# A fused AdaLN block with a mixture of experts: low parts of the bias rows on VectorE, and new hand-written orders at both ends

## The reference

```
mod = silu(c) @ wmod                      # per batch: sa, ca, ga, sb, cb, gb (128 each)
ga, gb = sign * max(abs, 0.25)
h = layernorm(x) * (1 + ca) + sa
v, gate = split(h @ W_in + b_in)
hs[t] = sigmoid(A) * hs[t-1] + v[t]       # scan along the sequence
x = x + ga * ((sigmoid(gate) * hs * C) @ W_out + b_out)
h = layernorm(x) * (1 + cb) + sb
p = softmax(h @ gate_w + gate_b); p = p where p >= 0.1, else 0; w = p / sum(p)
x = x + gb * sum_e w_e * (h @ expert_w[e] + expert_b[e])
```

## Time and profile before

| what | value |
|---|---|
| median of 3 runs | 209.23 us (208.98 to 212.89) |
| the profiled execution | 209.71 us |
| its span, first to last instruction | 207.9 us |
| mean granted clock of TensorE | 0.985 |
| instructions | 4221 |

### The profile page before, as it was taken

One profiled execution on the slowest core, in us unless ns is written; L12 is line 12 of the kernel. 1 busy time (PEld: TensorE's weight loads), 2 busy tenths in 40 slices (PEclk: granted clock), 3 DMA queues, 4 the chain that ended last, 5 costly groups with the idle time before them and its releaser, 6 DMA issues.

```text
span 207.9 us, 4221 instructions
## 1 busy us (share of the span) xinstructions
PE 192.8 (93%) x951; PEld 142.7 (69%) x951; DVE 188.9 (91%) x840; ACT 180.5 (87%) x596; POOL 169.0 (81%) x216
## 2 busy tenths in 40 slices
PE   6998979999999999999999999999999999989930
PEld 6764358676776868686867787777778686667710
DVE  2878996999998999999999999999999999698994
ACT  3527259999999999999999999999999999999940
POOL 8158999677999898979898988898988948877860
PEclk9999999999999999999999999999999999999985
DMA  6710121301111111112111101111010101001103
GB/s 194 211 33 2 50 60 26 110 15 53 38 50 50 57 50 50 50 50 55 52 52 43 53 16 55 39 52 54 2 50 0 54 2 52 2 0 54 39 13 101
DMA packets 20114, 10.34 MB, mean 50 GB/s; under 512 B 1369, under 2 KB 19938, under 8 KB 20090
## 3 DMA queue, kind: packets, MB, share of 16 engines
q1 hardware_dynamic: 20072, 10.07, 17.0%
q10 hardware_dynamic: 18, 0.00, 0.0%
HBM read 5.81 MB, written 4.26 MB: 48 GB/s over the span
## 4 chain that ended last, share of the span: by engine, by line
PE 72%; ACT 12%; DVE 10%; issue 2%; DMA 2%; DVEq 0%; SPq 0%; ACTq 0%
PE ring L1790 11%; PE ring L1791 11%; PE ring L1792 11%; PE bank_a L1729 7%; PE bank_v L1714 7%; ACT z L718 6%; PE bank_g L1720 6%; PE bank_g L1766 3%; PE bank_a L1675 3%; PE bank_g L1765 3%; ACT xn L731 3%; PE bank_g L1675 2%; PE bank_v L1710 2%; DMA wmod<-in_L_wmod_dram 2%; PE bank_v L1807 1%
## 5 line engine op out<-in xcount | busy, mean ns | idle before, releaser
L718 ACT ACTIVATE z<-ring,wts 128x128 f32<-128x128 f32 x436 | 122.3, 414 | 2.6 <-PE ring L1792 1.1
L517 POOL TENSOR_TENSOR z<-z 128x512 f32<-128x512 f32 x45 | 59.3, 1322 | 15.7 <-ACT z L718 15.7
L1790 PE MATMUL ring<-expert_w_hi,h_hi 128*128 128x512 f32 x128 | 59.2, 463 | 0.1
L1792 PE MATMUL ring<-expert_w_hi,h_lo 128*128 128x512 f32 x128 | 50.6, 395 | 0.0
L1791 PE MATMUL ring<-expert_w_lo,h_hi 128*128 128x512 f32 x128 | 50.4, 394 | 0.0
L525 POOL TENSOR_TENSOR z<-z 128x512 f32<-128x512 f32 x31 | 39.7, 1297 | 5.5 <-DVE z L1053 5.2
L496 POOL TENSOR_SCALAR xn<-x_in,neg_mean,rstd 128x128 f32<-128x128 f32 x60 | 26.6, 458 | 6.9 <-DVE rstd L992 6.6
L1790 PEld LDWEIGHTS ring<-expert_w_hi,h_hi 128*128 128x128 f32 x128 | 24.2, 189 | 8.5 <-issue 4.2
L1791 PEld LDWEIGHTS ring<-expert_w_lo,h_hi 128*128 128x128 f32 x128 | 24.2, 189 | 6.7 <-issue 3.3
L1792 PEld LDWEIGHTS ring<-expert_w_hi,h_lo 128*128 128x128 f32 x128 | 24.1, 188 | 5.7
L731 ACT ACTIVATE xn<-x,shift,rstd 128x128 f32<-128x128 f32 x60 | 25.6, 558 | 0.0
(11 more groups left out here) (122 smaller groups left out, 384.6 us busy)
## 6 DMA issues: line engine op xcount, KB each, us to landing
x_in<-in_L_attn_x_dram SPq DMA_DIRECT2D x16, 256.0 KB, 2.8
out_dram<-x SPq DMA_DIRECT2D x15, 256.0 KB, 2.3
expert_w<-in_L_ffn_expert_w_dram SPq DMA_DIRECT2D x2, 256.0 KB, 3.9
wmod<-in_L_wmod_dram SPq DMA_DIRECT2D x1, 384.0 KB, 4.6
expert_b_parts<-b_hi SPq DMA_DIRECT2D x8, 32.0 KB
out_dram<-x SPq DMA_DIRECT2D x2, 128.0 KB, 1.9
w_in<-in_L_attn_W_in_dram SPq DMA_DIRECT2D x1, 128.0 KB, 4.9
expert_b_parts<-b_lo SPq DMA_DIRECT2D x4, 32.0 KB
```

Source lines behind the costliest of these rows:

```text
L517: nc.gpsimd.tensor_tensor(z[:, g % 2, t, 0:4, :], z[:, g % 2, t, 0:4, :], z[:, g % 2, t, 4:8, :], ALU.add).then_inc(folded[t], 1)
L718: last = nc.scalar.activation(z[:, g % 2, t, e, :], bank_k[:, (e % 4) * P:(e % 4 + 1) * P], ACT.Copy, scale=wts[:, g % 2, t, e:e + 1])
L1790: mm(bank_k[:, :], hi, expert_w_hi[:, cols], start=True, stop=False)
L1792: mm(bank_k[:, :], lo, expert_w_hi[:, cols], start=False, stop=True).then_inc(e_ready[k], 1)
```

## The change

VectorE makes the low part of the bias rows: two instructions of 8x512, `bias_rows_low(0)` and `(1)`, read the ring bank (PSUM) and the high part. ScalarE's copies, GpSimd's instruction, the tile expert_b_rows and the semaphore bias_copied are gone. SyncE and TensorE's after_rows wait for both low parts.

The written-out fill now goes up to step 5 (six groups) and the loop begins at step 6; the order of the calls is new on all four engines in the fill and in groups 12 to 15. The `keep_clock` calls are 5 + 5 + 1 ahead of group 0's products (before 6 + 1 + 2 + 2), and there are two new ones, of 4 and 5 matmuls, before turn_xn2(0) and before turn_xn1(2). Loop bodies are the same. The diff is cut; the left-out lines move calls of later groups.

```diff
--- before.py
+++ after.py
@@ -35,15 +35,17 @@
 DVE_HALVES = (7,)
 LAST_DVE_HALVES = {14: (3, 7), 15: (3, 5, 7)}
 LAST_DVE_PAIRS = (1,)
-FIRST_HALVES = ((0, 5), (0, 0), (0, 6), (0, 2), (0, 1), (0, 4), (0, 3), (0, 7), (1, 6), (1, 0), (1,
-                2), (1, 1), (1, 5), (1, 4), (1, 3), (1, 7), (2, 4), (2, 0), (2, 5), (2, 3), (2, 2),
-                (2, 1), (2, 6), (3, 6), (2, 7), (3, 2), (3, 3), (3, 5), (3, 0))
+FIRST_HALVES = ((0, 0), (0, 5), (0, 4), (0, 1), (0, 6), (0, 2), (0, 7), (0, 3), (1, 0), (1, 4), (1,
+                5), (1, 1), (1, 6), (1, 3), (1, 7), (1, 2), (2, 4), (2, 1), (2, 0), (2, 6), (2, 2),
+                (2, 5), (2, 7), (2, 3), (3, 2), (3, 6), (3, 3), (3, 0), (3, 4), (3, 1), (3, 5), (3,
+                7), (4, 6), (4, 2), (4, 3), (4, 4), (4, 0), (4, 5), (4, 1), (4, 7), (5, 6), (5, 2),
+                (5, 3), (5, 5), (5, 0))
 HALF_ORDER = ((4, -1), (1, -1), (7, -1), (6, 0), (2, 0), (3, 0), (5, 0), (0, 0))
-HALF_STEPS = (4, 12)
-LAST_HALVES = ((11, 4), (11, 1), (11, 7), (12, 6), (12, 5), (12, 3), (12, 1), (12, 4), (12, 7), (12,
-               0), (12, 2), (13, 2), (13, 0), (13, 6), (13, 3), (13, 4), (13, 5), (13, 7), (13, 1),
-               (14, 5), (14, 6), (14, 2), (14, 7), (14, 4), (14, 0), (14, 3), (14, 1), (15, 2), (15,
-               4), (15, 6), (15, 5), (15, 7), (15, 1), (15, 3), (15, 0))
+HALF_STEPS = (6, 12)
+LAST_HALVES = ((11, 4), (11, 1), (11, 7), (12, 6), (12, 0), (12, 5), (12, 4), (12, 1), (12, 2), (12,
+               3), (13, 2), (13, 6), (12, 7), (13, 0), (13, 3), (13, 5), (13, 4), (13, 7), (13, 1),
+               (14, 2), (14, 6), (14, 4), (14, 7), (14, 5), (14, 0), (14, 3), (14, 1), (15, 4), (15,
+               6), (15, 5), (15, 2), (15, 7), (15, 1), (15, 0), (15, 3))
 
@@ -85,7 +87,6 @@
         expert_w_hi = sb("expert_w_hi", [P, experts * P], F32R)
         expert_w_lo = sb("expert_w_lo", [P, experts * P], F32R)
         expert_b = sb("expert_b", [batches, experts * P])
-        expert_b_rows = sb("expert_b_rows", [batches, experts * P])
         expert_b_hi = sb("expert_b_hi", [batches, experts * P], F32R)
         expert_b_lo = sb("expert_b_lo", [batches, experts * P], F32R)
...
@@ -360,7 +360,7 @@
 
                 sp.wait_ge(bias_rows_ready, 2)
                 sp.dma_start(b_hi_d, expert_b_hi[:, :].bitcast(F32)).then_inc(bias_written, 16)
-                sp.wait_ge(bias_low_ready, 1)
+                sp.wait_ge(bias_low_ready, 2)
                 sp.dma_start(b_lo_d, expert_b_lo[:, :].bitcast(F32)).then_inc(bias_written, 16)
                 sp.wait_ge(bias_written, 16 * 2)
                 sp.wait_ge(zeroed[2], batches)
@@ -476,12 +476,6 @@
                                         b_out[:, :].unsqueeze(1).to_broadcast([P, 2, P]),
                                         ALU.mult).then_inc(gab_ready, 1)
 
-            def expert_bias_low():
-                pool.wait_ge(bias_rows_ready, 2)
-                pool.wait_ge(bias_copied, 2)
-                nc.gpsimd.tensor_tensor(expert_b_lo[:, :], expert_b_rows[:, :], expert_b_hi[:, :].bitcast(F32),
-                                        ALU.subtract).then_inc(bias_low_ready, 1)
-
             def gate_low():
...
@@ -527,58 +521,73 @@
 
             identity()
             clear_expert_b(0)
-            clear_expert_b(1)
             clear_pick()
             clear_parts()
-            clear_expert_b(2)
-            clear_expert_b(3)
+            clear_expert_b(1)
             v_bias()
             first_norm(1)
-            clear_expert_b(4)
-            clear_expert_b(5)
+            clear_expert_b(2)
             gab(0)
             out_weights(0)
             biased_input(0)
+            biased_input(1)
             expert_low()
-            biased_input(1)
             gate_low()
+            first_norm(2)
+            gab(1)
+            clear_expert_b(3)
+            out_weights(1)
+            clear_expert_b(4)
+            clear_expert_b(5)
+            gab(2)
+            biased_input(2)
             clear_expert_b(6)
-            first_norm(2)
-            out_weights(1)
+            first_norm(3)
             out_weights(2)
-            biased_input(2)
-            expert_bias_low()
-            first_norm(3)
-            gab(1)
-            weight_parts(0)
             clear_expert_b(7)
-            gab(2)
-            gab(3)
             biased_input(3)
...
@@ -659,11 +668,6 @@
                 act.wait_ge(bias_rows_done, 1)
                 nc.scalar.copy(expert_b_hi[:, h * 512:(h + 1) * 512],
                                ring[h][0:batches, :]).then_inc(bias_rows_ready, 1)
-
-            def bias_rows_copy(h):
-                act.wait_ge(bias_rows_done, 1)
-                nc.scalar.copy(expert_b_rows[:, h * 512:(h + 1) * 512],
-                               ring[h][0:batches, :]).then_inc(bias_copied, 1)
 
             def skip_columns():
                 act.wait_ge(w_out_in, 16)
@@ -736,72 +740,96 @@
             load_condition()
             tanh_of_cond()
             load_state_bias()
+            pick_rows(0)
             silu_columns()
-            pick_rows(0)
+            pick_rows(1)
             vectors()
-            skip_columns()
-            pick_rows(1)
             h1(0)
             gate(0)
+            skip_columns()
             gates_out(0)
             h1(1)
+            gates_out(1)
             expert_high()
-            gates_out(1)
             gates_out(2)
             gate(1)
-            bias_rows_copy(0)
+            bias_rows_high(0)
+            bias_rows_high(1)
             gate_rows_high()
-            bias_rows_high(0)
             h2_high(0)
-            bias_rows_copy(1)
+            gates_out(3)
             h1(2)
-            bias_rows_high(1)
             exponentials(0)
-            gates_out(3)
             gate(2)
             second_norm(1)
+            weigh(0, 0)
             weigh(0, 5)
-            weigh(0, 0)
             h2_high(1)
-            weigh(0, 6)
             weigh(0, 1)
             h1(3)
             weigh(0, 4)
+            weigh(0, 6)
             exponentials(1)
             weigh(0, 2)
             gate(3)
+            weigh(0, 3)
             second_norm(2)
-            weigh(0, 3)
+            weigh(1, 0)
             parts_out(0)
             h2_high(2)
+            weigh(1, 4)
+            weigh(1, 5)
+            h1(4)
+            weigh(1, 1)
+            exponentials(2)
...
             exponentials(15)
             parts_out(13)
             weigh(14, 0)
             weigh(14, 1)
-            weigh(15, 2)
             weigh(15, 4)
             weigh(15, 6)
+            weigh(15, 2)
             parts_out(14)
             weigh(15, 1)
             parts_out(15)
@@ -912,6 +940,12 @@
             def decays():
                 dve.wait_ge(vectors_ready, 1)
                 vec.tensor_scalar(decay[:, :], a_tanh[:, :], 0.5, 0.5, ALU.mult, ALU.add).then_inc(decay_ready, 1)
+
+            def bias_rows_low(h):
+                dve.wait_ge(bias_rows_ready, h + 1)
+                cols = slice(h * 512, (h + 1) * 512)
+                vec.tensor_tensor(expert_b_lo[:, cols], ring[h][0:batches, :], expert_b_hi[:, cols].bitcast(F32),
+                                  ALU.subtract).then_inc(bias_low_ready, 1)
 
             def gate_rows_low():
                 dve.wait_ge(gate_rows_ready, 1)
@@ -1189,58 +1223,57 @@
                 last.then_inc(xn2_ready, 1)
 
             clear_moments()
+            silu()
             x_stats(0, 0)
             x_stats(0, 1)
-            silu()
             x_stats(0, 2)
             x_stats(0, 3)
             moments(-2)
             root(-2, 0)
             root(-2, 1)
             root(-2, 2)
+            negated_mean(-2)
             root(-2, 3)
-            negated_mean(-2)
             root(-2, 4)
             root(-2, 5)
+            root(-2, 6)
             root(-2, 7)
-            root(-2, 6)
-            modulation(0)
+            root(-2, 8)
+            first_norm(0)
             x_stats(1, 0)
             x_stats(1, 1)
             x_stats(1, 2)
             x_stats(1, 3)
-            root(-2, 8)
             moments(-1)
-            first_norm(0)
+            modulation(0)
             root(-1, 0)
-            guarded_gates()
             root(-1, 1)
+            negated_mean(-1)
             root(-1, 2)
-            negated_mean(-1)
             root(-1, 3)
             root(-1, 4)
+            guarded_gates()
             root(-1, 5)
             root(-1, 6)
             root(-1, 7)
+            root(-1, 8)
             modulation(1)
-            root(-1, 8)
+            gate_parts()
+            decays()
             x_stats(2, 0)
-            gate_parts()
             x_stats(2, 1)
-            decays()
+            x_stats(2, 2)
             scan(0)
+            x_stats(3, 0)
             gated(0)
-            x_stats(3, 0)
+            x_stats(2, 3)
             x_stats(3, 1)
-            x_stats(2, 2)
             x_stats(3, 2)
-            x_stats(2, 3)
             scan(1)
```

(56 more changed lines are left out.)

561 lines of the change are left out of this document (360 added, 201 removed).

## The result

| kernel | executions | median us | lowest to highest |
|---|---|---|---|
| before | 20 | 209.25 | 208.13 to 212.89 |
| changed | 20 | 207.53 | 207.26 to 209.33 |

The ratio of changed to before is 0.9942 (0.9923 to 0.9961), so 1.2 us less, within 2% of no change. It leaves out executions of a kernel that lie over 1.5% above its fastest, as those of before from 211.6 us on, which is part of why the medians stand 1.7 us apart. The forecast was 208.2 us. The profiled execution of the changed kernel took 207.48 us (209.71 before), its span 205.6 us (207.9).

What follows compares the result with a forecast made beforehand. No single engine bounds the kernel: three are busy 87 to 93%, and only the 32 us outside the unchanged steps can move. 209.71 - 0.4 (fill) - 0.3 (groups 1 to 5) - 0.3 (drain) = 208.7 profiled, 208.2 median; range 206.0 to 210.6.

Steps and rivals of the forecast that it cites:

- groups 1 to 5: From the first weighing to the steady loop: 0.3 of the 1.15 us lost comes back (0.8 worse to 1.15 better).
- the drain: End of the kernel: 0.3 of ScalarE's 0.39 us wait before its last weighings is gained (0.8 worse to 1.0 better).
- The two copies and GpSimd's subtraction at 0: Fill: removing ScalarE's two 0.57 us copies and GpSimd's 2.35 us instruction gains 0, as other waits cover them.
- VectorE's subtractions: Fill, ahead of shifts(1), scan(2) and group 0's last router step: 0.69 us each, together 1.4 us (1.2 to 2.2).
- Net about 0.9 us later: VectorE at scan(2): delay from the added subtractions after two moved x_stats and gaps are set against them.
- TensorE's wait at after_rows: Fill: second low part ends about 29.8 us, TensorE arrives about 30.2, so the wait costs 0.
- The first group: Ahead of 16 us: earlier norm, h1(0) at 9.4, scan at 13.5 to 14.3, x1(0) 0.6 to 1.6 us earlier.
- rival (a): Start of the fill: clock rises earlier, from about 6 us; with other terms at good ends 206.2 us; chance 0.18.
- the price of the order of the first group: Fill: gate_rows, the gates' copy and h1(1) come earlier, taken as 1.0 us at x1 of group 0.
- The first weighing: End of the fill: ScalarE's weighings start at 32.65 instead of 33.09 us, 0.4 gained (0.6 loss to 1.2 gain).
- (b): Fill and loop: subtractions eat the first group's gain, the steady loop absorbs the rest; 209.2 us, chance 0.22.
- (c): Fill: group 0's weights come 1.3 us late behind the subtractions, delaying weighings; 210.8 us, chance 0.18.

Runs made afterwards that it cites:

- low_undone: Changed kernel with the low parts made as before (two ScalarE copies, one GpSimd subtraction), all else in the new order; ratio to before 0.9945.
- low_only: Kernel before with VectorE making the low parts, without the copies and GpSimd's instruction, other calls in the old order; ratio to before 1.0043.
- early_keep_old: Changed kernel with the early keep_clock calls as before (6 and 1 around turn_silu instead of 5 and 5); ratio to before 0.9991.
- no_late_keep: Changed kernel without the two late keep_clock calls (4 and 5 matmuls); ratio to before 0.9945, executions 207.14 to 212.32 us.
- drain_pool_old: Changed kernel with only GpSimd's drain (groups 11 to 15) in the old order; ratio to before 1.0517, 220.38 us.
- drain_only: Kernel before with the changed drain alone (groups 11 to 15 in the new order on all four engines); ratio to before 0.9943.
- tail_only: Kernel before with only the change's last stretch: last halves swapped, VectorE's new order from weigh_onto(15, 5, 0) on; ratio to before 1.0001.

## Why the prediction was right or wrong

The time came 0.7 us under the forecast and inside the range, and the sign was right. The steps under it are another matter: 0.7 us were forecast for the fill and groups 1 to 5, where at most 0.25 came, and 0.3 for the drain, which gave 1.2. The two errors cancelled, and that the sum came out is luck.

- *The two copies and GpSimd's subtraction at 0*: not contradicted. low_undone, which puts them back and takes VectorE's work away, has 0.9945 beside 0.9942.
- *VectorE's subtractions*: 0.69 us each predicted, 0.66 and 0.67 measured. "Net about 0.9 us later" is what happens in the old order: in low_only the weights come 13.46 us behind x1, 12.60 before. In the new order VectorE is not last there, so the ledger that took this amount from the fill's gain charged something that was hidden. What the prediction did not have is their price in the loop: it expected the distance from group 8 to group 15 unchanged, and one step grew by 0.36 us.
- *TensorE's wait at after_rows*: none, as predicted. The second low part ended at 28.72 us, the first half stands on the chain from 29.34.
- *The first group*: every mark came earlier than written. first_norm(0) ended at 7.54 (7.9 predicted), h1(0) started at 8.89 (9.4), the scan at 12.93 (13.5 to 14.3), x1(0) came 1.95 us earlier (0.6 to 1.6). This is rival (a): the clock was up from about 6.3 us. The reason it gives, the longer unbroken run of keep_clocks, fits early_keep_old, but is not enough: no_late_keep and drain_pool_old have the same ten, and their clock rose later. Rival (a)'s doubt, that VectorE's queue would let through only 0.5 of TensorE's 2 us, was wrong in the profile.
- **The step that failed: the price of the order of the first group.** The forecast took 1.0 us at x1(0) for it against a profile in which the clock rose late, and wrote that down to the order of calls. drain_only, with the old order and an early clock, is 0.27 us behind. Of the 1.95 us in the profiles some 1.7 are thus the clock of that one execution; with the clock late in both, the lead is 0.2 to 0.3. In compared executions the fill is worth nothing (1.0008).
- *The first weighing* 0.4 earlier: 1.5 in the profiles, for the same reason. keep_clock(bank_g, 4) at 0.85 us on the chain: 0.89.
- *Groups 1 to 5*, 0.3 back: 0.1 worse. The term was wrong, its size within its bounds.
- **The second step that failed: the drain**, 0.3 us taken "of the 0.39 us" before ScalarE's last weighings. It gave 1.2 us: the ratio of drain_only is that of the whole change; in the profiles 0.7 us come between group 14's transposes and the last half, and 0.5 behind it. The earlier trace rows showed only where the waiting ends. Much of the time was lost earlier, at 185 to 190 us, where TensorE was idle for 0.73 of 5 us and which the prediction's rows left out; TensorE's idle time up to the last half fell by 0.48 of the 0.7 us. Its thought that VectorE's queue would be late next was right: the swap of the halves is worth nothing without the rest (tail_only).
- *Rivals (b) and (c)*: their mechanism, the subtractions ahead of the router, is real in the old order (low_only). In the new order it costs nothing up to the first weighing.

By the rule of the skill cited in the prediction (the Trainium skill, "TensorE: Matmul & The Clock Gate", "What's actually happening"), the slow clock is the default and activity releases it. The profiles of early_keep_old and of the changed kernel agree with it: 1.91 us, behind an idle time of 1.70, against 0.86 for the same pair.

Left open: what VectorE does in the gap of 0.38 us that comes with the low parts; why the clock rises early in some executions and late in others of the same start; and whether the old order of the fill with the new early keep_clocks would do as well as the new one.

## What to carry to other kernels

Before a place in one profile is priced, see at which level the clock stood there: a pair that takes 1.73 us where its like takes 0.86 tells of this execution, and the same order with an early clock may have the gain already. Compare two profiles from a mark behind the rise of the clock to the next, as from x1 to the first weighing here, and not from the start. In hand-written orders over several engines a move is part of a set: parts of this drain gave 0 and 0.2%, the whole 0.57%, and one engine left in its old order cost 5%. To price a drain, look for the stretch in which the busiest engine stands still, not for the last wait of the chain. And look for what two added instructions do far away from their place: here they came with a gap 90 us later.

## What the runs showed of the hardware

- TensorE's clock fell to 1.2 GHz behind short idle times: 1.70 us after light work at the start (granted clock 0.80, then 0.52), and 1.05 and 1.20 us near 26 us (0.83 and 0.83; 0.82 and 0.50), there in some executions only.
- When the clock first rises differs between executions with the same start: with the new early keep_clocks x1 of group 0 lay at 17.43 to 19.20 us in eight profiles.
- The granted clock is no safe witness at the start: the earlier trace rows have 1.00 at 5 to 10 us, and the pair at 12.07 still took 1.73 us.
- A subtraction of 8x512 from PSUM took VectorE 0.66 us, as much as the 0.67 us of a 128x512 one.
- A sum on VectorE (128x256, two operands) that started beside a running GpSimd addition took 0.97 us in place of 0.42 and ended 0.28 us behind it; a pair of them took 1.82 in place of 0.74.
- With two more instructions on VectorE in the fill, one gap of 0.38 to 0.40 us without a visible cause stood in the loop, in eight of eight profiles; without them in none of six.
